# Attention outputs of a two-attention, expert kernel: rows moved through DRAM and scaled by broadcast inverse sums, where they were turned to tokens and back on TensorE

## The reference, cut to what matters

```python
# x: (8, 512, 256). Each of the 8 batches is independent.
h = _layernorm(x) * (1 + ca) + sa
x = x + ga * attn_1(h)                 # 16 heads of width 16, causal
h = _layernorm(x) * (1 + cb) + sb
x = x + gb * ffn(h)

def attn_1(in_features):
    scores = jnp.einsum('bhqd,bhkd->bhqk', q, k) / sqrt(d_k) + mask
    attn = jax.nn.softmax(scores, axis=-1)
    out = jnp.einsum('bhqk,bhkd->bhqd', attn, v)
    ...
    return jnp.einsum('bsv,mv->bsm', out, o_proj_weight)

def ffn(x):                            # x: (8, 512, 256)
    q, k, v of layernorm(x)            # 32 heads of width 8, not causal
    p = jax.nn.softmax(att, axis=-1)
    o = jnp.einsum('bhqk,bkhd->bqhd', p, v).reshape(B, S, D) @ wo + x
    h = jax.nn.gelu(einsum('metd,edf->metf', xe, w1) + b1)
    return einsum('metf,efd->metd', h, w2) + b2
```

## Time and profile before

| | |
|---|---|
| median of 3 runs | 1618.95 us (1614.46 to 1720.31) |
| the profiled execution, its own time | 1617.25 us |
| its span, from the first to the last instruction | 1615.5 us |
| granted TensorE clock, mean | 0.978 |
| busy: PE, DVE, ACT, POOL | 1480.6, 1178.6, 1006.5, 528.6 us |
| moved by DMA | 170.48 MB, the mean busy share of 16 engines 0.38 |

### The profile page before, as it was taken

One profiled execution on the slowest core, in us unless ns is written; L12 is line 12 of the kernel. 1 busy time (PEld: TensorE's weight loads), 2 busy tenths in 40 slices (PEclk: granted clock), 3 DMA queues, 4 the chain that ended last, 5 costly groups with the idle time before them and its releaser, 6 DMA issues.

```text
span 1615.5 us, 30373 instructions
## 1 busy us (share of the span) xinstructions
PE 1480.6 (92%) x10001; PEld 643.3 (40%) x10001; DVE 1178.6 (73%) x2989; ACT 1006.5 (62%) x2096; POOL 528.6 (33%) x1218
## 2 busy tenths in 40 slices
PE   6685889989999999999999999999999989999977
PEld 4232423333434334343444334343344334344325
DVE  6667489768787787868787787877878688866610
ACT  1152456765767667675766767676767666777761
POOL 4232345144432243414443244414343134211100
PEclk9698899999999999999999999999999999999989
DMA  6851333453434352534444352444425221522111
GB/s 192 211 132 34 118 96 99 95 140 112 109 110 121 74 141 73 146 98 126 103 125 106 87 149 73 134 115 125 103 76 142 68 72 51 156 59 87 60 34 65
DMA packets 136743, 170.48 MB, mean 106 GB/s; under 512 B 16968, under 2 KB 102280, under 8 KB 136592
## 3 DMA queue, kind: packets, MB, share of 16 engines
q1 hardware_dynamic: 130704, 164.17, 36.8%
q10 hardware_dynamic: 5888, 4.37, 1.0%
HBM read 110.67 MB, written 56.66 MB: 104 GB/s over the span
## 4 chain that ended last, share of the span: by engine, by line
PE 77%; DVE 10%; ACT 6%; issue 3%; DMA 2%; POOL 1%; SPq 1%; POOLq 0%; ACTq 0%; DVEq 0%
PE bank_out L1333 19%; PE bank_scores L1314 13%; PE bank_max L1284 10%; PE bank_side L1247 7%; PE bank_side L1414 7%; PE bank_side L1257 4%; PE bank_max L1343 3%; PE bank_max L1398 3%; DVE neg_max L1555 3%; ACT probs L1107 2%; PE bank_side L1379 2%; PE bank_side L1370 2%; PE bank_side L1398 2%; DVE bank_max L1552 2%; PE bank_scores L1398 2%
## 5 line engine op out<-in xcount | busy, mean ns | idle before, releaser
L1107 ACT ACTIVATE probs<-bank_scores 128x512 f32<-128x512 f32 (+3 forms) x1536 | 752.4, 543 | 332.0 <-PE bank_scores L1314 322.2
L1555 DVE TENSOR_REDUCE neg_max<-bank_max 128x1 f32<-128x512 f32 x1024 | 655.9, 683 | 113.3 <-PE bank_max L1284 109.4
L1333 PE MATMUL bank_out<-probs,v_tile 128*9 128x512 f32 (+4 forms) x3072 | 363.5, 545 | 6.2 <-ACT out_raw L1120 2.6
L1284 PE MATMUL bank_max<-k_stack,q_stack 64*128 64x512 bf16 (+3 forms) x2048 | 312.1, 341 | 41.6 <-DVE neg_max L1552 17.4
L1314 PE MATMUL bank_scores<-q_stack,k_stack 64*128 64x512 bf16 (+3 forms) x2048 | 315.5, 345 | 32.4 <-ACT probs L1107 32.0
L1552 DVE CUSTOM_DVE_ANT_0 bank_max<-bank_max,causal 128x384 f32<-128x384 f32 (+3 forms) x512 | 241.7, 514 | 103.3 <-PE bank_max L1284 100.5
L1314 PEld LDWEIGHTS bank_scores<-q_stack,k_stack 64*128 64x128 bf16 x2048 | 80.6, 93 | 317.6 <-issue 305.8
L957 POOL CAST max_parts<-max_row 16x128 bf16<-16x128 f32 x96 | 27.6, 288 | 479.2 <-DVE max_row L1566 479.2
L1284 PEld LDWEIGHTS bank_max<-k_stack,q_stack 64*128 64x128 bf16 x2048 | 103.5, 95 | 117.4 <-issue 76.2
L1414 PE MATMUL bank_side<-w_out,hidden_T 128*128 128x256 f32 x512 | 140.9, 401 | 3.2 <-issue 1.1
L975 POOL TENSOR_SCALAR_AFFINE_SELECT probs<-probs 128x512 f32<-128x512 f32 x128 | 81.3, 636 | 140.7 <-ACT probs L1107 140.6
(11 more groups left out here) (149 smaller groups left out, 1543.8 us busy)
## 6 DMA issues: line engine op xcount, KB each, us to landing
q_stack<-q_parts SPq DMA_DIRECT2D x124, 256.0 KB, 4.3
k_stack<-k_parts SPq DMA_DIRECT2D x122, 192.0 KB, 5.8
w_in<-in_L_ffn_w_dram SPq DMA_DIRECT2D x16, 1024.0 KB, 4.9
w_out<-in_L_ffn_w_dram SPq DMA_DIRECT2D x16, 1024.0 KB, 5.9
q_parts<-partsq SPq DMA_DIRECT2D x32, 384.0 KB, 3.1
k_parts<-partsk SPq DMA_DIRECT2D x32, 384.0 KB, 2.6
q_parts<-partsq SPq DMA_DIRECT2D x32, 256.0 KB, 3.1
k_parts<-partsk SPq DMA_DIRECT2D x32, 256.0 KB, 3.1
```

What stands on the lines that cost most here:

```text
L1107: nc.scalar.activation(probs[s % 2][:, head_at(k), q0:S], region[bank][:, q0:S], ACT.Exp, scale=float(WIDTH[a]) ** -0.5).then_inc(drained[ ...
L1284: ins = pe.matmul(region[to][:, 0:keys], q_stack[buf][rows, at, qt * P:(qt + 1) * P], k_stack[buf][rows, at, 0:keys], start=(i == 0), stop ...
L1333: ins = pe.matmul(outb[32 * k:32 * k + WIDTH[a] + 1, q0:S], v_tile[a][:, kt, g * GROUP + k, :], probs[s % 2][:, k, q0:S], start=(kt == 0), ...
L1555: v.tensor_reduce(dst, region[bank], AX_X, ALU.max).then_inc(drained[bank], 1)
```

## The change

For 70 of the 96 groups (attention 0: groups 0 and 1 of batches 1 to 7; attention 1: all groups of batches 0 to 6) `normalise` is left out, and for 21 of the 32 `head_features` as well. In their place:

- `sums_out`: SP stores `out_raw` (128x512 f32, 256 KB) to DRAM.
- `load_sums`: two DMAs for a half of a batch: the sum rows, spread over 128 partitions (128x64 for attention 1, 128x32 for attention 0) into `sums_T`, and the output rows, 128x512, straight into `heads_T[a][:, cc, :]`.
- `invert`: DVE takes the reciprocal of `sums_T`.
- `store_inverse`, `load_inverse`: the inverse sums go to DRAM and come back broadcast over the rows of each head as 128x512, `inverse_T`.
- `scale_heads`: DVE multiplies `heads_T` by `inverse_T`.

There are 21 such halves, and 18 + 8 groups are turned on the chip as before. Each pass has three: (n, 1, 0), (n+2, 0, 0) and (n, 1, 1), written as (batch, attention, half). `qk` items and `ffn_sum` move by up to two steps in the passes and the tail, `ffn_sum` of batch 0 by three and more.

```diff
+def turned_on_chip(b, a, g):
+    if a == 0:
+        return b == 0 or g >= HEADS[0] // GROUP // 2
+    return b == BATCHES - 1
...
+def heads_items(b, a, cc):
+    return [(kind, b, a, cc) for kind in ("load_sums", "invert", "store_inverse", "load_inverse", "scale_heads")]
...
 def place_pass(plan, first, n):
-    place_units(plan, first, (23, 31), [("head_features", b, 0, 0), ("head_features", b, 0, 1)])
+    place_units(plan, first, (23,), [("head_features", b, 0, 1)])
     place_units(plan, first, (33, 43, 53, 63), out_items(b))
+    place_units(plan, first, (181, 201, 201, 213, 231), heads_items(n, 1, 0))
+    place_units(plan, first, (261, 281, 281, 293, 313), heads_items(n + 2, 0, 0))
+    place_units(plan, first, (413, 433, 433, 443, 461), heads_items(n, 1, 1))
...
-        place_units(plan, first, (393, 403, 411, 421, 431, 441, 451, 481), qk_items(0, n + 3))
+        place_units(plan, first, (393, 403, 411, 421, 431, 441, 451, 461), qk_items(0, n + 3))
...
-    place_units(plan, first, (433, 443), [("head_features", n, 1, 0), ("head_features", n, 1, 1)])
-    place_units(plan, first, (453, 461), in_pieces("ffn_sum", n, 0))
-    place_units(plan, first, (471, 473), in_pieces("ffn_sum", n, 1))
-    place_units(plan, first, (471, 482), [("bias_columns", n), ("keep_x", n + 1)])
+    place_units(plan, first, (463, 471), in_pieces("ffn_sum", n, 0))
+    place_units(plan, first, (473, 481), in_pieces("ffn_sum", n, 1))
+    place_units(plan, first, (471, 502), [("bias_columns", n), ("keep_x", n + 1)])
...
+            def sums_out(b, f, a, s):
+                g = s // T
+                if turned_on_chip(b, a, g):
+                    return
...
+                wait(sp, drained["out"], group_number[b, a, g] + 1)
+                sp.dma_start(raw_dram[a][g], out_raw[:, g % 2, :]).then_inc(raw_stored[a][g % 2], 16)
...
+            def load_sums(b, f, a, cc):
+                last = HEADS[a] // GROUP // C * (cc + 1) - 1
+                for g in (last - 1, last):
+                    wait(sp, raw_stored[a][g % 2], stored(b, a, g))
+                wait(sp, inverse_stored, 16 * scaled_number[b, a, cc])
+                side_read(a)
+                columns = HEADS[a] // C * S // P
+                rows = rows_of(a, cc)
+                sp.dma_start(sums_T[:, 0:columns], rows[:, WIDTH[a], :].rearrange("h (c e) -> h c e", e=columns)).then_inc(sums_loaded, 16)
+                sp.dma_start(heads_T[a][:, cc, :], rows[:, 0:WIDTH[a], :]).then_inc(heads_loaded[a], 16)
+
+            def store_inverse(b, f, a, cc):
+                wait(sp, inverse_made, scaled_number[b, a, cc] + 1)
+                columns = HEADS[a] // C * S // P
+                sp.dma_start(inverse_dram[a][cc].rearrange("h (c e) -> (h c) e", e=columns), sums_T[:, 0:columns]).then_inc(inverse_stored, 16)
+
+            def load_inverse(b, f, a, cc):
+                n = scaled_number[b, a, cc]
+                wait(sp, inverse_stored, 16 * (n + 1))
+                wait(sp, heads_made, n)
+                src = inverse_dram[a][cc].unsqueeze(1).broadcast_to([HEADS[a] // C, WIDTH[a], S])
+                sp.dma_start(inverse_T[:, :], src).then_inc(inverse_loaded, 16)
...
+            def invert(b, f, a, cc):
+                n = scaled_number[b, a, cc]
+                wait(dve, sums_loaded, 16 * (n + 1))
+                columns = HEADS[a] // C * S // P
+                v.reciprocal(sums_T[:, 0:columns], sums_T[:, 0:columns]).then_inc(inverse_made, 1)
+
+            def scale_heads(b, f, a, cc):
+                n = scaled_number[b, a, cc]
+                wait(dve, heads_loaded[a], 16 * (loaded_chunks[a].index((b, cc)) + 1))
+                wait(dve, inverse_loaded, 16 * (n + 1))
+                v.tensor_tensor(heads_T[a][:, cc, :], heads_T[a][:, cc, :], inverse_T[:, :], ALU.mult).then_inc(heads_made, 1)
```

135 lines of the change are left out of this document (98 added, 37 removed).

## The result

| | before | after |
|---|---|---|
| median of the runs | 1618.59 us | 1687.14 us (1677.06 to 1687.45) |
| ratio | | 1.0417, 95% interval 1.0366 to 1.0469 |
| span of the profiled execution | 1615.5 us | 1685.7 us |
| granted TensorE clock, mean | 0.978 | 0.946 |
| PE busy | 1480.6 us | 1466.6 us |

The ratio leaves out one run of the kernel before, of 1720.31 us, which fell in a slower state of the chip. The change makes the kernel 4.2% slower. The forecast was 1642 us: no change by its own bound of 2%, where the kernel is 68.5 us slower. 1687 lies 2 us beyond the upper end of its range.

A forecast was written before the change was run, and what follows sets the result against it. PE was taken as the bound in the passes. -52.4 + 33.5 + 7.5 + 15 + 9 + 5 + 5 = +22.6 us on 1617.25 made 1639.9, and 1642 us as the median; range for 8 in 10: 1588 to 1685.

The forecast's parts named there:

- the clock: PE's granted clock falls to half once a pass, after the (n+2, 0, 0) wait: 9 us (0 to 27).
- the short wait at (n, 1, 0): VectorE waits 1.2 to 2.4 us for the inverses before the multiply; PE loses 1.5 a pass, 7.5 us (0 to 12).
- SP's own waits: On SP's queue they hold up max rows needed three steps later, over 9 us; nothing was taken for it.
- work saved, less VectorE's lumps: Removed transposes and a shorter PE wait save 52.4 us; added VectorE reciprocals and multiplies cost 5 (0 to 15).
- long wait, (n+2, 0, 0), with a clock fall: Sums land behind the stack load; VectorE waits 7.1 us, PE loses 6.7 a pass: 33.5 us (17 to 42), clock 9.
- (n, 1, 1), multiply: VectorE waits 3.4 us for the inverses before the multiply; PE loses some 3.0 a pass, 15 us (0 to 24).
- first pass: First pass and tail: seven more round trips with a short wait here and there, 5 us (0 to 12).
- rival 2: No queueing for small loads: a DMA needs 2.3 to 2.7 us wherever it is issued; 1600 us, chance 0.13.
- the 3.0 of a copy: PE's 0.6 us wait a pass for ACT's copy before the first `attention_out` goes, as that turn comes earlier: 3.0 us saved.
- L1718's idle time: Sign in the profile after: 30 to 45 us idle before this line, released by the DMA of `sums_T`.
- rival 3: Slower: the DMA queue itself binds, all three waits at upper bounds, each bringing the clock down; 1694 us, chance 0.20.
- Rival 1: Hidden round trips: loads land within their two steps, only VectorE's lumps stay; 1572 us, chance 0.12.

The follow-up runs named there:

- e8: Changed kernel without its DRAM stores, loads and their waits; reciprocals and multiplies stay, scaling of attention outputs is missing: 1575.48 us.
- e1: Changed kernel with (n+2, 0, 0)'s inversion, inverse store, inverse load and multiply placed later in the five middle passes: 1644.31 us.
- e3: e1 with the multiply of (n, 1, 0) moved from place 231 to 253 in the middle passes and the last: 1619.65 us.
- e4: e3 with the multiply of (n, 1, 1) moved from place 461 to 491 and the `ffn_sum` pieces behind it: 1603.68 us.
- e6: e4 with (n+2, 0, 0)'s inverse load moved from place 343 to 353, and (n, 1, 1)'s multiply later in the last pass: 1603.53 us.
- e9: e6 with the inverse load of (n, 1, 1) moved from place 443 to 463, behind the max rows: 1597.99 us.
- e10: e8 with the 70 stores of raw rows and ScalarE's waits for them back; still incomplete: 1579.53 us.
- e11: e9 with first-pass items later: inversion, store, inverse load and multiply of (0, 1, 1), and multiply of (1, 0, 0): 1590.43 us.
- e5: Kernel before plus, in each middle pass, a load of 16 bytes a partition and a VectorE wait for it; no transposes removed: 1656.42 us.

## Why the prediction was wrong

The direction of the net was right (waits outweigh the saved transposes) and so was the mechanism, three in-order waits of VectorE. What failed are two sizes, the clock and the short wait at (n, 1, 0), and one step that was put at nothing, SP's own waits. The kernels, laid one behind the other, account for the whole difference:

| step of the prediction | predicted us | by the medians | by the ratios | by |
|---|---|---|---|---|
| work saved, less VectorE's lumps | -47.4 | -39.1 | -39 | before to e8 |
| long wait, (n+2, 0, 0), with a clock fall | 33.5 + 9 | 42.8 | 40 | after to e1 |
| (n, 1, 0), multiply | 7.5 | 24.7 | 22 | e1 to e3, six waits |
| (n, 1, 1), multiply | 15 | 16.0 | 17 | e3 to e4 |
| SP's waits | 0 | 5.5 | 7 | e6 to e9 |
| stores' traffic | no term | 4.1 | 0.5 | e8 to e10 |
| first pass | 5, with the tail | 7.6 | 8 | e9 to e11 |
| not attributed | | 11 | 13 | e11 to e10 |

The ratios are those against the kernel before beside each, times 1616 us. Both columns telescope: the medians add up to 72.6, which is 1687.14 less the 1614.56 of the kernel before in the round of e8, the ratios to the 4.2% of the result. Each step is measured with the others as they stood then; another order could share them out otherwise.

The profiled executions split the same difference into what PE did. The last two columns are read from the clock in each trace: PE's busy time while the granted clock stood at 1.2 GHz, and the number of such stretches in the five passes.

| kernel | span, us | PE busy | PE idle | busy at half clock | stretches |
|---|---|---|---|---|---|
| before | 1615.5 | 1480.6 | 134.9 | 46 | 0 |
| changed | 1685.7 | 1466.6 | 219.1 | 122 | 14 |
| e1, long wait gone | 1642.9 | 1451.9 | 191.0 | 91 | 9 |
| e3, and (n, 1, 0) | 1617.5 | 1445.7 | 171.8 | 73 | 5 |
| e4, and (n, 1, 1) | 1600.9 | 1436.8 | 164.1 | 58 | 2 |
| e8, no round trip | 1573.0 | 1431.3 | 141.7 | 47 | 0 |

**The long wait was right.** Predicted was a wait of 7.1 us and a PE loss of 6.7 from the landing of 6.9 us in the earlier trace rows; the mean of the five is 7.4, and PE's pause 6.9. (Its upper bound of 8.4 was a slip: 689.0 + 8.4 gives a loss of 8.1.) The choice against rival 2 was right as well: 2 KB landed in 7.1 us behind the stack load. The Trainium skill's "DMA: Bandwidth & Descriptors", in the section on queues, rings and completion order, says that each DMA engine consumes descriptors in ring order; the trace agrees, with 7.1 us there and 1.4 us for 16 KB on a free queue. The fixed part of some 2 us that the same page gives in the anatomy of one DMA, for the GpSimd path, is no guide to a landing on SP's queue while that is in use.

**The clock was the most mis-sized term.** The step said "One fall a pass, after the long wait", 9 us, on one fall that the earlier trace rows shows behind a pause of 2.46 us. There were 14 falls in the five passes. By that same row the pause of some 3.0 us that the prediction itself gave PE at (n, 1, 1) had to bring a fall too. As the waits were taken away one kind at a time, the falls beside them went with them: 14, 9, 5, 2 and 0. (The row was also read a little long: 0.79 in the microsecond from 109 puts the end of the half clock at 109.4 and not 109.8, which makes 1.7 us a fall; e5 measured 1.8.) The same 9637 instructions take 1466.6 us in the changed kernel and 1431.3 without the round trip: 35.3 us more, over two thirds of what the transposes had saved (1480.6 less 1431.3 is 49.3). That this is the clock, the busy time at half clock bears out: it is 75 us more, and what 75 us do at half speed takes some 37 at full speed.

The span's 70.2 us are then 49.3 saved, 35.3 given back to slower matmuls, and 84.2 of added idle time. In the prediction's sum the same three are 49.4 saved (52.4 less the 3.0 of a copy, which is idle time), 9 for the clock and 63.0 of added idle time. So of the 47.6 us by which it fell short of the span, 26 are the clock and 21 idle time.

**The multiply of (n, 1, 0)** was put at 1.5 us for PE and measured 3.7 to 4.1 a time. VectorE's wait of 2.5 us lies just above the bound of 2.4. PE stood for 2.8 us in the pass shown, since the drain of `bank_side` was behind the multiply; from e1 to e3 its idle time fell by 3.2 us a time and its busy time, the clock's part, by 1.0.

**(n, 1, 1)** came out as summed by luck in part. Of the 15 us, all put at idle time, e3 to e4 shows 7.7 as idle and 8.9 as busy time, the clock that the term didn't have. VectorE's waits were 3.89, 6.19, 5.53, 2.88 and 2.14 us where 3.4 was forecast, and e4 gave part of the gain back by its late max rows (PE's waits for them are 10.3 us in e4 and 5.7 in e3).

**"SP's own waits in between hold up the max rows behind them, but these are needed three steps later, over 9 us; I take nothing for it"** was false as a step: moving one such load gave 5.5 us. It hid behind the three larger waits while these were there (4.2 us of PE's waits in the changed kernel), and came up as they went: 10.3 us in e4. Not all of these waits are SP's, though: e10, with the stores alone, has 6.3 us of them.

**The saved work** came through as counted: PE's busy time fell by 49.3 us from before to e8. What didn't come through went into idle time, which rose by 6.8 us (134.9 to 141.7, of it 0.4 a pass, so mostly outside the passes); the prediction had a rise of 5 for lumps and a fall of 3.0 for the copy. The spans differ by 42.5 us, the medians by 39.1.

**The signs.** Borne out: L1718's idle time of 43.1 us (30 to 45), L1725's of 8.7 us in the pass shown (5 to 10), PE waiting at L1405 (59.0 us), and 104 transposes at L1464. Not borne out: a pass of 188.5 us, where 197.9 stands beyond even rival 3's 195, and PE's busy time lower by some 50 us, where it is lower by 14.0. The second is what should have been worked out ahead: if PE is slowed behind each pause, its busy time can't fall by the saved work.

**The rivals.** Rival 1 named the ceiling, 1572, well (1575.5). Rival 3 came near the size (1694), and its part that each of the three waits brings the clock down holds. Its reason, that the queue itself binds, does not: the stores cost 4 us at most, and e4 with the same traffic is faster than before. That its two conditions were coupled into one case of 0.20 left too little weight on the clock.

**Left open.** By the medians 11 us lie between e11 and e10, which has no loads, inverses or waits for them. PE's waits for max rows are 3.2 us in e11 and 6.3 in e10, so it is not these. Between the spans of the profiled executions it is 7.6 us. Cut at the first reciprocal of each pass, e11 has 3.4 less in the first pass, 3.4 more in the five passes together and 7.6 more from there to the end (224.1 against 216.5). So it lies in the tail, and what makes it there was not tried.

## What to carry to other kernels

A wait that is put into the list of an engine feeding the bottleneck costs what is left of the time from issue to landing, as the queue stands at that place, and then again a part in TensorE's clock: here 1.1 to 1.2 us for each microsecond of the long waits, and about 4 us for a wait of only 2.5. Before trading TensorE's work for a round trip through DRAM, list what is issued ahead of each hop (here eight DMAs of a stack load), and place the consumer behind the landing, not two steps behind the issue. And look past the consumer: an issuing queue that waits for a store, so as to load it again, holds up whatever stands behind it, and this shows only when the larger waits are gone.
